# Attention in two layers: the scores a second time, transposed, for one exponential per unit; the band mask on GpSimd

## Chip, cores and metric

The kernel runs on one core of a Trainium2 chip. The metric is the device time of one execution in microseconds (us). The engines run side by side and meet through semaphores: TensorE (PE; its weight loads are PEld), VectorE (DVE), ScalarE (ACT), GpSimd (POOL) and SyncE (SP), which issues most DMAs.

## The reference, cut to what matters

Two blocks follow each other, each with an attention and a feed-forward part; x is (16, 128, 1024).

```
x = x + tanh(g_xattn[0]) * _L0_xattn_ref(_layernorm(x), ctx, ctx, ...)
x = x + tanh(g_ffn[0])   * _L0_ffn_ref(_layernorm(x), ...)
x = x + tanh(g_xattn[1]) * _L1_xattn_ref(_layernorm(x), ctx, ...)
x = x + tanh(g_ffn[1])   * _L1_ffn_ref(_layernorm(x), ...)
# _L0_xattn_ref, per batch, for 16 heads x 4 states (64 "heads" of 16 dimensions), 128 x 128:
scores = einsum('bhqdm,bhkdm->bhqkm', qh, kh) / sqrt(dk)
weights = softmax(scores, axis=3)
out = einsum('bhqkm,bhkdm->bhqdm', weights, vh)
# _L1_xattn_ref: channels as sequence of T = 1024, 8 heads of 16, a window of 16 keys round each query:
dots = einsum('bhdt,bhdtw->bhtw', qh, k_win) * scale     # padded keys are zeros
attn = softmax(dots, axis=-1)
out = einsum('bhtw,bhdtw->bhdt', attn, v_win)
```

## The kernel before

`program` runs seven stages, one after another with a barrier between: setup, `project_q`, `project_kv`, `attention0`, `ffn0_project1`, `attend1`, `select_ffn1`. Both attentions are the function `attend` (lines 725 to 1037). It works in units of 8 heads: layer 0 has 128 units (16 batches of 8) of 128 queries and 128 keys; layer 1 has 144 (16 batches of 9 tiles), a tile being 113 queries (121 in the first, 112 in the last) against the 128 keys that hold their windows.

For a unit u, with the queries on the partitions: `score` (PE) multiplies `qs` and `ks`, both split into high and low parts that lie on 64 partitions, into `s_bank`, 8 matmuls of 128 columns into two of PSUM's banks; in layer 1 two bf16 matmuls of 512 columns first lay down the band of 0 and -1e30. `maximum` (DVE) reduces the 8 rows of scores to their negated maxima `nmax`. `exponential` (ACT) needs one op per head, since its bias is that head's column of `nmax`: 8 ops into `probs`. `turn` (PE) transposes the 8 blocks into `t_bank`; `turn_out` copies them to `pt`, half by DVE and half by ACT. `value` (PE) multiplies them with `vpad`, V padded to 32 columns with a column of ones, so that the sum of each row of probabilities comes along, dimensions on the partitions, into `o_bank`; `value_out` (DVE) copies to `osb`; `turn_back` (PE) transposes that into `b_bank`, queries on the partitions again; `divide` (DVE) takes reciprocals of the sums and multiplies into `att`, which SP stores once a batch. In layer 1 the first and last tile of a batch (edges) also count the padded keys, `raw`, `low`, `epad` and `den`.

The order on each engine is written out by `staggered(eng, units, per_loop, stages)`: in step c, an engine runs its listed functions in order, each for unit c + lead. PE has score at lead 4, turn at 2, value at 1, turn_back at 0, and the other engines have matching lists:

```
staggered(pe, B * upb, un.per_loop, [(4, score), (2, turn), (1, value), (0, turn_back)])
staggered(dve, B * upb, un.per_loop, [(4, maximum), (2, turn_out), (1, value_out), (0, divide)])
staggered(act, B * upb, un.per_loop, [(3, exponential), (2, turn_out)])
```

An engine's list is strictly in order: a wait in it holds everything after it. `done(t)` is the semaphore's value when unit t is finished, `free(t, depth)` when the buffer that unit t reuses is. `s_bank`, `probs` and `pt` have two buffers, `t_bank`, `o_bank` and `b_bank` one. SP loads `qs` and `ks` from DRAM (2 MB for four units of layer 0, 4 MB for a batch of layer 1; two slots) and V, and GpSimd copies V into `vpad` once a batch; in layer 0 it also loads and splits the next stage's weight. `project_kv` (line 579) and `ffn0_project1` (line 1238) write K and Q to DRAM in high and low parts.

## Time and profile before

| | us |
|---|---|
| Median of 3 runs | 2406.85 (2403.96 to 2409.03) |
| The profiled execution | 2407.05, its span 2405.4 |
| PE busy | 2182.1 (91%) |
| DVE busy | 1394.1 (58%) |
| ACT busy | 975.4 (41%) |
| POOL busy | 174.0 (7%) |
| Granted clock of PE, mean | 0.956 of 2.4 GHz |

The page splits the span into 40 slices of 60 us. The stage of layer 0's attention is at slices 12 to 17, that of layer 1's at slices 27 to 34; in both, three engines are busy for most of a slice, outside them ScalarE hardly is. Durations are those of the profiled execution. The end of a matmul is modelled, so for PE the distance from the start of one block to the start of the next is the better measure of what a block takes.

### The profile page before, as it was taken

The numbers are of one execution on the slowest core, as the hardware profiler recorded it, in microseconds if no ns is written. First come the engines' busy times: TensorE is split into PE (matmuls) and PEld (weight loads), VectorE is DVE, ScalarE is ACT, GpSimd is POOL, SyncE is SP. The second block draws the span as 40 slices with busy tenths as digits, with TensorE's granted clock in tenths as the row PEclk, the third lists the DMA queues.
The fourth block names the chain that finished last, engine by engine and source line by source line (L and its number), as shares of the span: only waits on it lengthen the run. The fifth ranks groups of instructions, "written<-read, shape, count | busy, mean of one in ns | idle before, by whom it ended". The sixth has DMA issues, their size and how long they took to land. (4 is left out here: it accounts for less than half of the span.)

```text
span 2405.4 us, 49290 instructions
## 1 busy us (share of the span) xinstructions
PE 2182.1 (91%) x17638; PEld 1766.2 (73%) x17638; DVE 1394.1 (58%) x2604; ACT 975.4 (41%) x2850; POOL 174.0 (7%) x225
## 2 busy tenths in 40 slices
PE   5999699999979999979978999959999996775998
PEld 4999689989957777758854777737777774564887
DVE  4443322112159999923325777649999995784664
ACT  2222221111059999900002111129999995440000
POOL 0000000000021212100000000010000000330000
PEclk9999899999989999989988999979999998886999
DMA  3223533332356777533323878775655653751221
GB/s 126 106 105 123 172 135 132 140 148 113 131 229 260 273 276 267 197 140 131 131 96 128 304 291 314 277 303 183 241 195 195 238 186 96 247 175 58 87 86 58
DMA packets 163583, 426.59 MB, mean 177 GB/s; under 512 B 14192, under 2 KB 90736, under 8 KB 151216
## 3 DMA queue, kind: packets, MB, share of 16 engines
q1 hardware_dynamic: 161200, 417.16, 47.2%
q0 software_dynamic: 2304, 8.39, 1.1%
q8 instruction: 48, 0.79, 0.1%
q14 instruction: 31, 0.25, 0.0%
HBM read 257.73 MB, written 167.77 MB: 177 GB/s over the span
## 5 line engine op out<-in xcount | busy, mean ns | idle before, releaser
L953 ACT ACTIVATE a_probs<-a_s_bank,a_nmax 128x128 f32<-128x128 f32 (+3 forms) x2176 | 598.8, 422 | 36.0 <-DVE a_nmax L893 36.0
L893 DVE TENSOR_REDUCE a_nmax<-a_s_bank 128x8 f32<-128x1024 f32 (+1 forms) x240 | 293.5, 1223 | 47.5 <-PE a_s_bank L999 23.8
L1009 PE MATMUL a_t_bank<-ident_sb,a_probs 128*128 128x128 f32 (+3 forms) x2176 | 286.2, 275 | 1.1 <-ACT a_pt L961 0.8
L1009 PEld LDWEIGHTS a_t_bank<-ident_sb,a_probs 128*128 128x128 f32 (+3 forms) x2176 | 225.0, 142 | 21.0 <-ACT a_probs L953 1.1
L907 DVE COPY a_pt<-a_t_bank 128x512 f32<-128x512 f32 (+3 forms) x272 | 177.1, 651 | 4.3 <-PE a_t_bank L1009 4.3
L961 ACT ACTIVATE a_pt<-a_t_bank 128x512 f32<-128x512 f32 (+3 forms) x272 | 165.0, 606 | 29.0 <-PE a_t_bank L1009 27.4
L1024 PE MATMUL a_o_bank<-a_pt,a_vpad 128*32 128x128 f32 (+3 forms) x4352 | 168.8, 273 | 0.5 <-DVE a_osb L914 0.5
L373 PE MATMUL q_qb<-q_xt_hi,wq_hi 128*128 128x256 f32 x512 | 145.5, 284 | 3.0 <-DVE wq_lo L248 3.0
L373 PE MATMUL kv_kb<-kv_ct_hi,wk_hi 128*128 128x256 f32 x512 | 145.0, 283 | 3.0 <-DVE wv_lo L248 3.0
L373 PE MATMUL kv_kb<-kv_ct_lo,wk_hi 128*128 128x256 f32 x512 | 144.9, 283 | 0.0
L373 PE MATMUL kv_kb<-kv_ct_hi,wk_lo 128*128 128x256 f32 x512 | 144.9, 283 | 0.0
L373 PE MATMUL q_qb<-q_xt_lo,wq_hi 128*128 128x256 f32 x512 | 144.8, 283 | 0.0
L373 PE MATMUL q_qb<-q_xt_hi,wq_lo 128*128 128x256 f32 x512 | 144.8, 283 | 0.0
L1024 PEld LDWEIGHTS a_o_bank<-a_pt,a_vpad 128*32 128x32 f32 x4352 | 99.1, 109 | 42.8 <-issue 23.8
L1351 ACT ACTIVATE f_shared<-f_banks,p_b 128x1024 fp32r<-128x1024 f32 x32 | 35.7, 1116 | 223.8 <-PE f_banks L1400 223.8
L1034 PE MATMUL a_b_bank<-ident_sb,a_osb 128*113 128x128 f32 (+1 forms) x544 | 123.8, 309 | 1.4 <-DVE a_att L936 1.4
L373 PE MATMUL f_banks<-f_hi,f_xt_hi 128*128 128x512 f32 x256 | 105.0, 410 | 7.2 <-DVE f_xt_lo L1295 7.2
L999 PEld LDWEIGHTS a_s_bank<-a_ks,a_qs 64*113 64x113 f32 (+2 forms) x1152 | 69.3, 177 | 57.2 <-issue 57.2
L987 PE MATMUL a_s_bank<-a_band,a_identb 128*113 128x512 bf16 (+2 forms) x288 | 87.2, 385 | 24.9 <-DMA a_ks<-k 22.6
L914 DVE COPY a_osb<-a_o_bank 128x256 f32<-128x256 f32 (+3 forms) x272 | 108.7, 400 | 1.0 <-PE a_o_bank L1024 1.0
L618 DVE TENSOR_TENSOR kv_raw<-kv_vb,bvf 128x512 f32<-128x512 f32 x32 | 22.1, 692 | 149.7 <-PE kv_vb L373 149.7
L612 DVE SCALAR_TENSOR_TENSOR kv_k_lo<-kv_kb,bkf,kv_raw 128x256 fp32r<-128x256 f32 x64 | 31.0, 484 | 133.5 <-ACT kv_raw L639 133.5
(200 smaller groups left out, 4563.6 us busy)
## 6 DMA issues: line engine op xcount, KB each, us to landing
a_qs<-q SPq DMA_DIRECT2D x32, 1024.0 KB, 6.1
a_ks<-k SPq DMA_DIRECT2D x32, 1024.0 KB, 8.1
k<-f_shared SPq DMA_DIRECT2D x64, 512.0 KB, 4.2
a_qs<-q SPq DMA_DIRECT2D x16, 2048.0 KB, 7.8
a_ks<-k SPq DMA_DIRECT2D x16, 2048.0 KB, 11.9
k<-kv_raw SPq DMA_DIRECT2D x32, 512.0 KB, 4.8
k<-kv_k_lo SPq DMA_DIRECT2D x32, 512.0 KB, 4.8
a_vraw<-v SPq DMA_DIRECT2D x32, 512.0 KB, 10.4
```

Of the source, the lines that this page charges most:

```text
L373: m = pe.matmul(out, a(x, c), b(y, c), start=(i + j == 0), stop=(len(terms) * j + i == n - 1))
L893: dve.tensor_reduce(nmax[0:m, k, :], scores(s)[0:m], X, ALU.max, negate=True).then_inc(maxed, 1)
L907: dve.tensor_copy(pt[:, k, 0:512].rearrange("p (h t) -> p h t", h=4)[:, :, 0:m], t_bank[:, 0, :].rearrange("p (h t) -> p h t", h=4)[:, :, ...
L914: dve.tensor_copy(osb[:, k, :].rearrange("p (g t) -> p g t", g=2)[:, :, 0:m], o_bank[:, 0, 0:2 * P].rearrange("p (g t) -> p g t", g=2)[:, ...
L953: a = act.activation(probs[0:m, k, h, :], scores(s)[0:m, h, :], ACT.Exp, bias=nmax[0:m, k, h:h + 1])
L961: act.activation(pt[:, k, 512:1024].rearrange("p (h t) -> p h t", h=4)[:, :, 0:m], t_bank[:, 1, :].rearrange("p (h t) -> p h t", h=4)[:, : ...
L987: pe.matmul(s_bank[0:m, 2 * k + bank, :], identb[:, 0:m], band[:, kind, :, :].rearrange("p h t -> p (h t)"), start=True, stop=False, skip_ ...
L999: a = pe.matmul(out, qs[at, slot, j, t0:t0 + m], ks[at, slot, j, w0:w0 + P], start=False, stop=True, skip_group_check=True)
L1009: a = pe.transpose(t_bank[:, h // 4, h % 4 * P:h % 4 * P + m], probs[0:m, k, h, :], e.ident[0:m, 0:m])
L1024: a = pe.matmul(o_bank[32 * j:32 * j + 32, 0, g * P:g * P + m], vpad[:, slot, UH * (s % upb) + head(h), :], pt[:, k, h * P:h * P + m], sta ...
L1034: a = pe.transpose(b_bank[0:m, 0, g * P:(g + 1) * P], osb[:, k, g * P:g * P + m], e.ident[:])
L1351: act.activation(halves(qk[j][0][:, s % 2, :]), pb, ACT.Identity, bias=b[:, j:j + 1]).then_inc(hi[j], 1)
```

## The change

In both attentions each unit's scores are computed twice. The first pass is as before, but with one buffer and only for the maxima. The maxima of a group of units (4 in layer 0, 3 in layer 1) are transposed by PE (`turn_max`), copied by ACT (`shift`) and written by a DMA that ACT issues into the rows 0 and 64 of `qs`, which are high parts' partners of rows of ones in `ks`: one DMA per group in layer 0, one per tile in layer 1. The second pass (`score_t`) has keys on the partitions and the queries as columns, and subtracts the maxima by those rows; one exponential per unit then writes `pt` directly. `turn`, `probs` and both `turn_out` go. `value_out` moves from DVE to ACT. In layer 1 the band is applied to `pt` after the exponential by GpSimd (`mask`), a multiplication of the bits, as integers, with 0 or 1; the band matmuls of the first pass stay. Tiles of layer 1 have 112 queries (120 in the first and last). `pt` has three buffers in layer 1, `qs` and `ks` four slots. The pipeline is deeper: score runs 9 units ahead. DRAM's K gets rows of ones, written in setup, and K is stored in five pieces instead of four, with the order of high and low parts swapped. The stores of layer 1's `att` are three instead of five. Values and division stay as they were in form.

```diff
 WIN, PADL = 16, 8
-TSTEP = P - WIN + 1
+TSTEP = P - WIN
 NT1 = 9
 NCL = 64
 QS = 0.25
 RAW = 4
-START = 16
+START = 32
...
+K_ROWS = ((0, slice(1, 16)), (0, slice(17, 32)), (1, slice(0, 32)), (2, slice(0, 32)), (3, slice(0, 32)))
+Q_ROWS = ((0, slice(0, 32)), (1, slice(0, 32)))
...
+            sp.wait_ge(unit_set, 1)
+            for k in (e.k0, e.k1):
+                sp.dma_start(k[:, 0:32:16, 0, :], unit[:]).then_inc(unit_out, 16)
+            sp.wait_ge(unit_out, 32)
+
+        @block.gpsimd
+        def _(pool):
+            pool.memset(unit[:], 1.0).then_inc(unit_set, 1)
...
-                    for j in range(4):
-                        sp.dma_start(e.k0[2 * g + b][:, j, :],
-                                     (k_hi, k_lo)[j % 2][:, b].rearrange("p o t -> p (o t)").bitcast(F32)
-                                     ).then_inc(k_out, 16)
+                    for j, r in K_ROWS:
+                        src = (k_lo, k_hi)[j % 2][4 * r.start:4 * r.stop, b].rearrange("p o t -> p (o t)")
+                        sp.dma_start(e.k0[2 * g + b][r, j, :], src.bitcast(F32)).then_inc(k_out, 16)
...
+        self.group = 4 if layer == 0 else 3
+        self.per_loop = 16 if layer == 0 else 36
+        self.batches = self.per_loop // self.per_batch
+        self.groups = self.per_loop // self.group
+        self.ahead = self.group + 4
...
+    G, L, upb = un.group, un.ahead, un.per_batch
+    R = UH * G
+    E = layer
+    D3 = 2 + E
...
-        s_bank = ps(n + "s_bank", [P, 4, 512]); t_bank = ps(n + "t_bank", [P, 2, 512])
-        o_bank = ps(n + "o_bank", [P, 1, 512]); b_bank = ps(n + "b_bank", [P, 1, 512])
-        v_zeroed = sem(n + "v_zeroed"); const = sem(n + "const")
-        qk_in = [sem(n + f"qk_in{k}") for k in range(2)]
+        s_bank = ps(n + "s_bank", [P, 2, 512]); st_bank = ps(n + "st_bank", [P, 4, 512])
+        b_bank = ps(n + "b_bank", [P, 1, 512]); o_bank = ps(n + "o_bank", [P, 1, 512])
...
+                slot, b = s // 4, un.batches * i + s // NU
+                sp.wait_ge(st_done, done(u - 13))
...
-                staggered(sp, B * upb, un.per_loop, [(0, store), (upb + 1, load_half), (upb + 1, load_values)])
+                staggered(sp, B * upb, un.per_loop, [(0, store), (14, load_half), (10, load_values)])
             else:
-                staggered(sp, B * upb, un.per_loop, [(0, store), (upb + 5, load_batch), (upb + 5, load_values)])
+                staggered(sp, B * upb, un.per_loop, [(0, store), (18, load_batch), (14, load_values)])
...
+            def mask(u, s, i):
+                m = un.rows(s)
+                kind = {None: 1, 0: 0, 1: 2}[un.edge(s)]
+                pool.wait_ge(expd, done(u))
+                p = pt[:, s % D3, :, 0:m]
+                pool.tensor_tensor(p.bitcast(I32), p.bitcast(I32), bandi[:, kind, 0:m].unsqueeze(1).to_broadcast([P, UH, m]),
+                                   ALU.mult).then_inc(masked, 1)
...
+            staggered(pool, B * upb, un.per_loop, [(2, mask), (6, batch_values)])
...
             def maximum(u, s, i):
-                m, k = un.rows(s), s % 2
+                m = un.rows(s)
                 dve.wait_ge(scored, done(u))
-                dve.wait_ge(expd, free(u))
+                to = nmax[0:m, s // G % 2, :].rearrange("p (a x) -> p a x", a=2)
+                if layer == 0:
+                    to = to[:, :, 4 * (s % 4):4 * (s % 4) + 4]
+                else:
+                    to = to.rearrange("p a (j t) -> p a t j", t=G)[:, :, s % G, :]
                 if un.edge(s) is None:
-                    dve.tensor_reduce(nmax[0:m, k, :], scores(s)[0:m], X, ALU.max, negate=True).then_inc(maxed, 1)
+                    dve.tensor_reduce(to, s_bank[0:m].rearrange("p b (h x) -> p b h x", h=4), X, ALU.max,
...
-            def turn_out(u, s, i):
-                m, k = un.rows(s), s % 2
-                dve.wait_ge(turned, done(u))
-                dve.wait_ge(valued, free(u))
-                dve.tensor_copy(pt[:, k, 0:512].rearrange("p (h t) -> p h t", h=4)[:, :, 0:m],
...
-            staggered(dve, B * upb, un.per_loop, [(4, maximum), (2, turn_out), (1, value_out), (0, divide)])
+            staggered(dve, B * upb, un.per_loop, [(L + 1 + E, maximum), (0, divide)])
...
             def exponential(u, s, i):
                 m, k = un.rows(s), s % 2
-                act.wait_ge(maxed, done(u))
-                act.wait_ge(turned, free(u))
-                if un.edge(s) is not None:
-                    act.activation(epad[0:m, un.edge(s), :], low[0:m, un.edge(s), :], ACT.Exp)
-                for h in range(UH):
-                    a = act.activation(probs[0:m, k, h, :], scores(s)[0:m, h, :], ACT.Exp,
-                                       bias=nmax[0:m, k, h:h + 1])
-                a.then_inc(expd, 1)
-
-            def turn_out(u, s, i):
+                act.wait_ge(st_done, done(u))
+                act.wait_ge(valued, free(u, D3))
+                act.activation(pt[:, s % D3, :, 0:m], by_head(st_bank[:, 2 * k:2 * k + 2, :])[:, :, 0:m],
+                               ACT.Exp).then_inc(expd, 1)
+
+            def shift(u, s, i):
+                if not un.group_last(s):
+                    return
+                g, k, mg = un.nth_group(s, i), s // G % 2, un.group_rows(s)
+                nth = un.groups // 2 * i + s // G // 2
+                act.wait_ge(turned, g + 1)
+                act.wait_ge(shift_in[k], 16 * shifts * nth)
+                act.activation(nrow[:, k, 0:mg], b_bank[0:R, 0, 2 * P:2 * P + mg], ACT.Copy).then_inc(rowed, 1)
+                act.wait_ge(rowed, g + 1)
+                if layer == 0:
+                    act.dma_start(qs[0:65:64, s // 4, :, :].bitcast(F32), nrow[:, k, :].bitcast(F32)).then_inc(shift_in[k], 16)
+                    return
+                for tile in range(G):
+                    slot, js, q, _ = place(s - s % G + tile)
+                    act.dma_start(qs[0:65:64, slot, :, q].bitcast(F32),
+                                  nrow[tile:R:G, k, 0:q.stop - q.start].bitcast(F32)).then_inc(shift_in[k], 16)
+
+            def value_out(u, s, i):
...
+            staggered(act, B * upb, un.per_loop, [(L + E, shift), (2 + E, exponential), (1, value_out), (4, pads)])
...
-                pe.wait_ge(expd, free(u))
+                elif un.first(s):
+                    pe.wait_ge(qk_in[slot], 32 * (i + 1))
+                pe.wait_ge(maxed, free(u, 1))
...
+            def turn_max(u, s, i):
+                if not un.group_last(s):
+                    return
+                g, mg = un.nth_group(s, i), un.group_rows(s)
+                pe.wait_ge(maxed, done(u))
+                pe.wait_ge(normed, done(u - L - E - 1))
+                pe.transpose(b_bank[0:R, 0, 2 * P:2 * P + mg], nmax[0:mg, s // G % 2, :].bitcast(F32),
+                             e.ident[0:mg, 0:mg]).then_inc(turned, 1)
+
+            def score_t(u, s, i):
+                slot, js, q, k = place(s)
+                m, st = un.rows(s), 2 * (s % 2)
+                if un.group_first(s):
+                    nth = un.groups // 2 * i + s // G // 2
+                    pe.wait_ge(shift_in[s // G % 2], 16 * shifts * (nth + 1))
+                pe.wait_ge(expd, free(u))
+                for j in range(4):
+                    for half in range(2):
+                        at = slice(64 * half, 64 * half + 64)
+                        a = pe.matmul(st_bank[:, st + half, j * P:j * P + m], ks[at, slot, js.start + j, k],
+                                      qs[at, slot, js.start + j, q], start=True, stop=True,
+                                      skip_group_check=True)
+                a.then_inc(st_done, 1)
...
-            staggered(pe, B * upb, un.per_loop, [(4, score), (2, turn), (1, value), (0, turn_back)])
+            staggered(pe, B * upb, un.per_loop, [(L + 1 + E, score), (2 + E, score_t), (L + E, turn_max), (1, value), (0, turn_back)])
```

## Rows read from the trace of the kernel before

**Rows 1.** The page's GB/s per slice; busy us (and count) by window, granted clock, DMA share, GB/s.
```profile
GB/s 126 106 105 123 172 135 132 140 148 113 131 229 260 273 276 267 197 140 131 131 96 128 304 291 314 277 303 183 241 195 195 238 186 96 247 175 58 87 86 58
...
core 0: us, PE busy (x) PEld busy (x) DVE busy (x) ACT busy (x) POOL busy (x), PEclk, DMA share, GB/s
...
700.00:1000.00 300.00, 296.69 (x3920) 226.13 (x3918) 289.35 (x579) 297.07 (x1044) 59.34 (x56) 0.99 0.70 264
...
1620.00:2000.00 380.00, 380.00 (x4836) 275.46 (x4828) 346.49 (x762) 356.27 (x1241) 19.14 (x30) 1.00 0.54 196
```
**Rows 2.** Timeline, first score block and last store of each attention stage: start us, duration us.
```profile
686.84 1.97 PE L995 MATMUL a_s_bank<-a_ks,a_qs 64*128 64x128 f32 x16 [12.36 <-DMA a_ks<-k]
...
1027.38 0.35 SPq L833 DMA_DIRECT2D att<-a_att  x1
...
1604.98 1.08 PE L987 MATMUL a_s_bank<-a_band,a_identb 128*121 128x512 bf16 x2 [22.65 <-DMA a_ks<-k]
...
2021.70 2.51 SPq L841 DMA_DIRECT2D att<-a_att  x5
```
**Rows 3.** Timeline of a step in layer 0's attention, PE and ACT.
```profile
802.19 0.65 ACT L961 ACTIVATE a_pt<-a_t_bank 128x512 f32<-128x512 f32 x1
...
802.66 0.44 PE L1034 MATMUL a_b_bank<-ident_sb,a_osb 128*128 128x128 f32 x2
802.68 2.22 ACT L953 ACTIVATE a_probs<-a_s_bank,a_nmax 128x128 f32<-128x128 f32 x8
...
803.03 0.66 PE L995 MATMUL a_s_bank<-a_ks,a_qs 64*128 64x128 f32 x8
...
803.62 1.09 PE L1009 MATMUL a_t_bank<-ident_sb,a_probs 128*128 128x128 f32 x8
...
804.64 0.65 PE L1024 MATMUL a_o_bank<-a_pt,a_vpad 128*32 128x128 f32 x16
...
805.22 0.44 PE L1034 MATMUL a_b_bank<-ident_sb,a_osb 128*128 128x128 f32 x2
```
**Rows 4.** Timeline of a step in layer 1's attention, PE and the maximum on DVE.
```profile
1801.58 0.59 PE L987 MATMUL a_s_bank<-a_band,a_identb 128*113 128x512 bf16 x2
...
1802.10 0.61 PE L999 MATMUL a_s_bank<-a_ks,a_qs 64*113 64x128 f32 x8
...
1802.64 0.99 PE L1009 MATMUL a_t_bank<-ident_sb,a_probs 113*128 113x113 f32 x8
1802.75 1.22 DVE L893 TENSOR_REDUCE a_nmax<-a_s_bank 113x8 f32<-113x1024 f32 x1 [0.32 <-PE a_s_bank L999]
...
1803.56 0.59 PE L1024 MATMUL a_o_bank<-a_pt,a_vpad 128*32 128x113 f32 x16
...
1804.09 0.47 PE L1034 MATMUL a_b_bank<-ident_sb,a_osb 128*113 128x128 f32 x2
...
1804.40 0.59 PE L987 MATMUL a_s_bank<-a_band,a_identb 128*113 128x512 bf16 x2
```
**Rows 5.** Timeline where layer 0's attention drains, with engines waiting.
```profile
1023.46 0.60 ACT L961 ACTIVATE a_pt<-a_t_bank 128x512 f32<-128x512 f32 x1 [1.25 <-PE a_t_bank L1009]
...
1024.07 0.42 DVE L914 COPY a_osb<-a_o_bank 128x256 f32<-128x256 f32 x1
...
1024.64 0.64 PE L1024 MATMUL a_o_bank<-a_pt,a_vpad 128*32 128x128 f32 x16 [0.27 <-DVE a_osb L914]
```
**Rows 6.** Groups by line and form: count, busy us in all, mean ns of one.
```profile
L1148 ACT ACTIVATE wo_xt_hi<-wo_tb 128x1024 fp32r<-128x1024 f32 x16 | 16.4, 1026 | 181.6 <-PE wo_tb L1164 181.6
...
L900 DVE TENSOR_SCALAR a_nmax<-a_raw,a_edges 112x8 f32<-112x8 f32 x15 | 3.4, 225 | 0.0
...
L360 POOL TENSOR_TENSOR wo_lo<-wo_raw,wo_hi 128x1024 f32 x8 | 18.9, 2359 | 0.0
```
**Rows 7.** Timeline of SyncE's queue in layer 1's attention, five stores of `att`.
```profile
1644.40 3.08 SPq L841 DMA_DIRECT2D att<-a_att  x5
```
**Rows 8.** By tile: landing of layer 0's `att` stores, then of GpSimd's `wo_raw` loads.
```profile
DMA to landing us min/median/max: 2.6/2.9/3.5
...
DMA to landing us min/median/max: 3.7/3.9/8.3
```

285 lines of the change are left out of this document (148 added, 137 removed).

## Prediction

> **What bounds the kernel now.** I read the page first: its rows of slices show that the work runs stage after stage (projections, attention of layer 0, a product, the low-rank product, attention of layer 1, selection, last product), so a change in one stage is worth what it does in that stage. The change touches the two attention stages. Busy time by window [rows 1] shows TensorE (PE) at 296.7 of 300 us of the first and 380.0 of 380 us of the second, at a granted clock of 0.99 and 1.00 of 2.4 GHz. ScalarE (297.1, 356.3) and VectorE (289.4, 346.5) are nearly as full, so no engine's time can be read as free until the others are counted. The stages last from their first score matmul to their last `att`: 686.8 to 1027.4 = 340.6 us, and 1605.0 to 2021.7 = 416.7 us [rows 2].
>
> Then the timeline of one step, where every PE block starts as the one before ends. Layer 0 [rows 3]: turn back 0.37 us (802.66 to 803.03), score 0.59, turn of the probabilities 1.02, value 0.58; a step is 2.56 us. Layer 1 [rows 4]: band matmuls 0.52, score 0.54, turn 0.92, value 0.53, turn back 0.31; a step is 2.82 us. With PE never idle, PE is the engine that sets the step, and the other two keep pace.
>
> **The change, part by part.**
>
> *PE, steady step.* The turn goes; a second score pass of the same form (eight 64-row matmuls) comes. Layer 0: its price is the score's 0.59, so a step is 0.58 + 0.37 + 0.59 + 0.59 = 2.13 us. Layer 1: between 0.54 and 0.59 [rows 3, 4]; I take 0.57, since the stationary side is 128 wide as in layer 0 and 112 columns move: 0.52 + 0.54 + 0.57 + 0.53 + 0.31 = 2.47 us. Once in a group (4 units in layer 0, 3 in layer 1) a small transpose of the maxima is added, half of the two-transpose turn back, 0.19 us. PE alone would give 2.18 and 2.53 us.
>
> *The maximum.* The scores now have one buffer, so score(u+1) waits for maximum(u), and all PE work queues behind it. The maximum starts 0.65 us after the score block starts and takes 1.23 [rows 4]; from the end of a VectorE op to the PE block that waits for it there are 0.15 us, of which the weight load takes the last 0.03 (1024.49 to 1024.64, [rows 5]); I use 0.12. Layer 0: 0.70 + 1.23 + 0.12 = 2.05, under 2.13, hidden with 0.08 to spare. Layer 1: 0.52 + 0.65 + 1.23 + 0.12 = 2.52, over 2.47, so a plain step is 2.52. Edge tiles (2 of 9) do one more small op of 0.225 [rows 6] before they report; in the one that doesn't fall in a slower step anyway this costs 0.33, or 0.04 a unit. VectorE loses both of its copies and keeps the maximum and two short ops: its sum is no bound.
>
> *ScalarE, throughput.* Eight exponentials and half of the copy become one exponential of 1024 (896) columns and the copy of the values. ScalarE takes 0.60 us for 512 columns and 1.026 for 1024 [rows 5, 6], so 0.92 for 896, 0.39 for 256, 0.36 for 224, and 0.28 for the 120 or 128 of the maxima. The next op starts 0.11 us before such a copy would end by itself: 0.49 after its start [rows 3]. That gives slots of 0.92 and 0.81 us for the exponential. About 1.3 us a step: no bound by its sum.
>
> *ScalarE, order.* This is the term that decides. Once a group ScalarE waits for the transpose of the maxima, which PE does in the middle of its step, copies the row (0.28), waits for that copy, and issues the DMA that puts it into `qs`: one in layer 0, three in layer 1. Behind it stand the exponential of that step and the copy of the values, and for that copy wait the next value block and turn back on PE. No row shows a DMA issued by ScalarE. SyncE's own: five stores with fixed addresses take 2.51 us, 0.50 each [rows 2]. Bounds are 0.35, the bare duration of one store [rows 2], and 0.62, five with computed addresses in 3.08 us [rows 7]. The addresses of the new DMAs are fixed: 0.50. With T the start of a group step on PE:
> Layer 0: score and second score to 1.18, transpose to 1.37, seen at 1.48; copied 1.81; issued 2.31; exponential to 3.23; values copied 3.62; seen by PE at 3.74. PE is ready for the next value block at 2.32 + 1.18 = 3.50. Stall 0.24. Average (4 x 2.13 + 0.19 + 0.24) / 4 = 2.24 us.
> Layer 1: band, score and second score to 1.63, transpose to 1.82, seen 1.93; copied 2.26; three issues to 3.76; exponential to 4.57; values copied 4.93; seen 5.05. PE is ready at 2.66 + 1.63 = 4.29. Stall 0.76. Average (2.66 + 2.47 + 0.76 + 2.52) / 3 = 2.80, with the edges 2.84 us. So layer 1's step stays at today's 2.82, although its matmuls shrink. With issues of 0.35 and 0.62 it would be 2.70 and 2.96.
>
> *GpSimd.* Layer 1's mask is one tensor_tensor of 896 columns per unit, behind the exponential and ahead of the value matmuls. The nearest row, two inputs and 1024 columns, takes 2.36 us [rows 6]: 2.06 for 896. The copy of V into its pad, 1152 columns a batch, adds at most 2.65 / 9 = 0.29. Some 2.4 us with waits, under 2.84; exponential to value has over two steps of room, as `pt` has three buffers. This row is fp32 and the mask is int32; a gain is excluded (the two reads stay), a loss isn't. The Trainium skill ("GPSIMD Engine Reference", Engine selection) advises against two-input elementwise work on this engine, as VectorE does it about twice as fast; by it the mask belongs on VectorE. The row says the mask fits, so the sum leaves it free; the rule's case is the first rival.
>
> *DMA.* The maxima arrive as 16 KB (layer 0), issued by T + 2.3 and needed by the second score three steps on, at about T + 7.3: 5.0 us; in layer 1 5.6 us. Stores of 512 KB land in 2.6 to 3.5 us [rows 8]. Layer 0's loads are the same bytes in less time: 264 GB/s [rows 1] becomes about 300, while single slices of the page show up to 314 [rows 1]. Hidden; a miss is the second rival. The five K stores instead of four, and the rows of ones in setup, lie on SyncE's queue beside PE work of other stages; I take 0, bounds 0 and 3 us.
>
> *Ends of the stages.* The pipeline is 9 units deep instead of 4. In the fill, PE mostly does scores alone, one maximum apart, and at about half speed, as in today's first blocks: band 1.08 us instead of 0.59 [rows 2, 4]. Layer 0: about 2.45 us a step, 22 in all; layer 1: six of 3.4 and three of 2.6, 28. Drain: layer 0 seven steps of 1.54 and two of 1.8, 14.4 us; layer 1 is held to GpSimd's 2.2 a unit, 18.
>
> *Sum.* Of the 128 + 9 and 144 + 9 steps, 119 and 135 are full ones. Layer 0: 22 + 119 x 2.24 + 14.4 = 303.0, against 340.6: -37.6. Layer 1: 28 + 135 x 2.84 + 18 = 429.4, against 416.7: +12.7. The rest: 0. Net -25: the profiled execution's 2407.05 (span 2405.4 and 1.65 around it; 0.2 above the median of the runs) gives 2382 us.
>
> **Rivals.**
> *The mask is slower than its fp32 relative* (a slower-ending case). GpSimd then sets layer 1's step from 2.5 us a mask on. At 3.2 us a step is about 3.5: 28 + 135 x 3.5 + 22 = 523 against 429, time 2476. For it: an integer product was never seen in this trace. Against: reading two inputs likely limits the row, not its arithmetic. Chance 0.15.
> *The maxima land late.* Each us beyond 5 costs 32 us in layer 0 (32 groups) and, beyond 5.6, 48 in layer 1. Landing in 6 us: 2382 + 32 + 19 = 2433. For it: a GpSimd load of 512 KB issued beside the first loads of the stage took 8.3 us. Against: the other loads of that line took 3.9 in the median beside loads as well [rows 8], and these transfers are 32 times smaller. Chance 0.12.
> *ScalarE's issues cost little* (0.1 us each). Layer 1's stall goes and its step is 2.61: 398 us, 31 less; layer 0 saves another 7: time 2344. Chance 0.15.
> *It doesn't do what it says*: the step stays PE's and PE does not speed up, because the second pass with weights 128 wide costs what the turn did (1.02, 0.92). Then 2.6 and 2.9 us: layer 0 346, layer 1 438, time 2434. Against: the first pass has the same form. Chance 0.05.
>
> **How the numbers follow.** Forecast 0.53, rivals as above. The forecast's own range, from the bounds of the issue (layer 1 -19 and +16, layer 0 -4 and +4), the fill (10 either way) and the K stores: 2350 to 2412. With the cheap issue below and the late landing above, 2338 to 2434 leaves out the slow mask and little else. Faster by over 0.2% (4.8 us, about what a measurement of this kernel can tell): 0.47 of the forecast, 0.15 of the cheap issue, 0.08 of a mask or a landing that misses only a little, 0.70. Same 0.08. Slower 0.22.
>
> **What the profile would show.** Layer 0's PE blocks at 2.13 us with a gap of 0.2 before every fourth value block; in layer 1 a gap of 0.8 before every third, released by ScalarE's copy of the values, with ScalarE standing in DMA issues before it. `nmax` reduce follows score at once. GpSimd at some 80% in layer 1 with masks near 2.1 us. Wrong if PE waits for the mask, if it waits for `qs` from `nrow`, if layer 1's stage is under 400 us, or if another stage moves by over 5 us.

## The result, and the profile after

The changed kernel takes 2722.75 us (median of 4 runs, 2705.31 to 2739.22), the kernel before 2407.94 beside it (4 runs, 2403.96 to 2410.29): 1.131 times as long, interval 1.123 to 1.138. The forecast was 2382 us, and the wider of its two ranges ended at 2434. The profiled execution spans 2716.1 us, 310.7 more than before.

The page of the changed kernel: its span, the busy sums, and of the slices the rows of PE, ACT, POOL, the clock and the DMA rate.

```profile
span 2716.1 us, 46746 instructions
...
PE 2429.7 (89%) x17718; PEld 1919.8 (71%) x17718; DVE 1210.9 (45%) x2060; ACT 640.9 (24%) x1026; POOL 476.2 (18%) x373
...
PE   5997899999799999979968999499888989685999
...
ACT  1221311110243434400001111023333333242000
POOL 0000000000211111100000000045565555332000
PEclk9999999999555555579989999657687575686999
...
GB/s 127 94 139 120 144 164 112 168 95 149 237 191 202 188 185 202 94 133 130 108 146 182 301 304 288 338 90 153 133 167 150 128 151 81 172 224 101 63 93 62
```

The row to stop at is PEclk, the clock that TensorE was granted, in tenths of 2.4 GHz. PE is as full in layer 0's attention (slices 10 to 16, counted from 0) as it was, but the clock is at 5 tenths for seven slices in a row, and it wanders between 5 and 8 in layer 1's (slices 26 to 34). Busy time by window, layer 0's stage and then layer 1's; columns as in [rows 1]:

```profile
686.60:1161.70 475.10, 463.91 (x4384) 344.21 (x4384) 220.52 (x384) 184.70 (x288) 66.26 (x63) 0.50 0.47 181
1743.70:2332.80 589.10, 527.42 (x5232) 360.48 (x5232) 290.77 (x528) 191.21 (x368) 322.12 (x176) 0.64 0.38 138
```

Layer 0's stage is 475.1 us instead of 340.6 [rows 2], at 0.50 of 2.4 GHz, the level of 1.2 GHz, instead of 0.99 [rows 1]: +134.5. Layer 1's is 589.1 instead of 416.7, at 0.64 instead of 1.00: +172.4. Together 306.9 of the 310.7 us; all the rest adds 3.8. PE is not waiting: from 720 to 1140 us it is busy for 420.00 of 420 us, at 0.50 throughout. ScalarE went from 297 busy us of 300 [rows 1] to 185 of 475, and VectorE from 289 of 300 to 221 of 475. The change did to them what it says.

A step of layer 0 in the timeline (start, duration):

```profile
900.35 0.69 PE L1117 MATMUL a_b_bank<-ident_sb,a_osb 128*128 128x128 f32 x2
...
900.97 1.11 PE L1065 MATMUL a_s_bank<-a_ks,a_qs 64*128 64x128 f32 x8
...
901.89 1.05 PE L1089 MATMUL a_st_bank<-a_qs,a_ks 64*128 64x128 f32 x8
...
902.87 1.08 PE L1103 MATMUL a_o_bank<-a_pt,a_vpad 128*32 128x128 f32 x16
902.98 1.02 ACT L1004 ACTIVATE a_pt<-a_st_bank 128x1024 f32<-128x1024 f32 x1 [2.11 <-PE a_st_bank L1089]
...
903.88 0.69 PE L1117 MATMUL a_b_bank<-ident_sb,a_osb 128*128 128x128 f32 x2
```

The four blocks are the forecast ones, back to back, and ScalarE had waited 2.11 us before its exponential. But each block takes 1.6 to 1.7 times its old length: score 0.92 (900.97 to 901.89) for 0.59, turn back 0.62 for 0.37, value 1.01 for 0.58 [rows 3]; the second score takes 0.98. The step is 3.53 us where 2.13 was forecast. It is PE's own clock, not a wait.

A group step of layer 1, in a stretch where the clock was up:

```profile
1986.95 0.25 ACT L1014 ACTIVATE a_nrow<-a_b_bank 24x112 fp32r<-24x112 f32 x1 [2.57 <-PE a_b_bank L1076]
1987.24 1.61 ACTq L1021 DMA_DIRECT2D a_qs<-a_nrow  x3
...
1989.01 0.97 ACT L1004 ACTIVATE a_pt<-a_st_bank 128x960 f32<-128x960 f32 x1 [1.81 <-issue]
1989.88 0.35 ACT L1028 ACTIVATE a_osb<-a_o_bank 128x224 f32<-128x224 f32 x1
1990.06 6.31 POOL L930 TENSOR_TENSOR a_pt<-a_pt,a_bandi 128x960 int32<-128x960 int32 x3 [3.79 <-ACT a_pt L1004]
...
1990.38 0.62 PE L1103 MATMUL a_o_bank<-a_pt,a_vpad 128*32 128x120 f32 x16 [1.17 <-ACT a_osb L1028]
```

This is the forecast's chain, line for line: row copied, three issues, exponential, values copied, and PE at the value block having waited for that copy: 1.17 us, forecast 0.76. (The tile in this step has 120 queries, hence 960 columns; the clock had come up at 1986.2 us.) By form, the masks: 2088 ns for 896 columns, 2.06 forecast.

```profile
L930 POOL TENSOR_TENSOR a_pt<-a_pt,a_bandi 128x896 int32<-128x896 int32 x112 | 232.1, 2088 | 166.4 <-ACT a_pt L1004 166.2
```

### The profile page after: what moved, and what is told of

Its sections match the earlier page's. It is cut to its first block and busy times, and to the rows that moved or that the text cites. A ratio compares the mean times of both kernels' runs of the same rounds, so it can differ in the third digit from the quotient of the medians.

```text
span 2716.1 us, 46746 instructions
## 1 busy us (share of the span) xinstructions
PE 2429.7 (89%) x17718; PEld 1919.8 (71%) x17718; DVE 1210.9 (45%) x2060; ACT 640.9 (24%) x1026; POOL 476.2 (18%) x373
## 5 line engine op out<-in xcount | busy, mean ns | idle before, releaser
L957 DVE TENSOR_REDUCE a_nmax<-a_s_bank 128x8 fp32r<-128x1024 f32 (+1 forms) x240 | 293.9, 1225 | 206.7 <-PE a_s_bank L1065 206.7
L1004 ACT ACTIVATE a_pt<-a_st_bank 128x1024 f32<-128x1024 f32 (+2 forms) x272 | 264.8, 974 | 417.8 <-PE a_st_bank L1089 307.2
L930 POOL TENSOR_TENSOR a_pt<-a_pt,a_bandi 128x896 int32<-128x896 int32 (+1 forms) x144 | 302.4, 2118 | 261.4 <-ACT a_pt L1004 261.0
L1065 PEld LDWEIGHTS a_s_bank<-a_ks,a_qs 64*128 64x128 f32 (+2 forms) x2176 | 220.8, 284 | 158.9 <-issue 150.0
L1065 PE MATMUL a_s_bank<-a_ks,a_qs 64*128 64x128 f32 (+2 forms) x2176 | 268.8, 390 | 26.0 <-DMA a_ks<-k 12.4
L1103 PE MATMUL a_o_bank<-a_pt,a_vpad 128*32 128x128 f32 (+2 forms) x4352 | 258.8, 381 | 17.1 <-ACT a_osb L1028 16.6
L1089 PE MATMUL a_st_bank<-a_qs,a_ks 64*128 64x128 f32 (+2 forms) x2176 | 261.9, 383 | 6.2 <-DMA a_qs<-a_nrow 6.2
L1089 PEld LDWEIGHTS a_st_bank<-a_qs,a_ks 64*128 64x128 f32 x2176 | 239.3, 301 | 11.4 <-issue 6.0
L1117 PE MATMUL a_b_bank<-ident_sb,a_osb 128*112 128x128 f32 (+1 forms) x544 | 172.5, 416 | 1.4 <-DVE a_att L990 1.4
L1059 PE MATMUL a_s_bank<-a_band,a_identb 128*112 128x512 bf16 (+1 forms) x288 | 131.3, 552 | 46.2 <-DMA a_ks<-k 25.2
```

Source lines behind the costliest of these rows:

```text
L930: pool.tensor_tensor(p.bitcast(I32), p.bitcast(I32), bandi[:, kind, 0:m].unsqueeze(1).to_broadcast([P, UH, m]), ALU.mult).then_inc(masked, 1)
L957: dve.tensor_reduce(to, s_bank[0:m].rearrange("p b (h x) -> p b h x", h=4), X, ALU.max, negate=True).then_inc(maxed, 1)
L1004: act.activation(pt[:, s % D3, :, 0:m], by_head(st_bank[:, 2 * k:2 * k + 2, :])[:, :, 0:m], ACT.Exp).then_inc(expd, 1)
L1059: pe.matmul(s_bank[0:m, bank, :], identb[:, 0:m], band[:, kind, :, :].rearrange("p h t -> p (h t)"), start=True, stop=False, skip_group_ch ...
L1065: a = pe.matmul(s_bank[0:m, half, j * P:(j + 1) * P], qs[at, slot, js.start + j, q], ks[at, slot, js.start + j, k], start=layer == 0, stop ...
L1089: a = pe.matmul(st_bank[:, st + half, j * P:j * P + m], ks[at, slot, js.start + j, k], qs[at, slot, js.start + j, q], start=True, stop=Tru ...
```

## The experiments

My theory after the first look: the granted clock falls because the turn of the probabilities is gone. It was PE's longest block, eight fp32 transposes on all 128 rows and columns of the array; what takes its place has matmuls on 64 rows. (Two such transposes stay, in the turn back, and in layer 1 the band matmuls, bf16 on 128 by 128.) Rivals: the level is lost at the stage's start and a push would bring it back; the stalls in the steps pull it down; the missing work of ScalarE and VectorE has to do with it.

For each kernel: its time, and length in us and granted clock of both attention stages. e4 and e8 are edits of the kernel before, all others of the changed one. From e1 to e12 each is one execution. The kernel before took 2404 to 2412 us in all of its executions beside them.

| kernel | time | layer 0 | layer 1 |
|---|---|---|---|
| before | 2407.94 | 340.6, 0.98 | 416.7, 0.99 |
| after | 2722.75 | 475.1, 0.50 | 589.1, 0.64 |
| e4_halfturn | 2520.56 | 455.7, 0.50 | 416.7, 0.99 |
| e8_quarterturn | 2434.97 | 364.3, 0.88 | 417.6, 0.98 |
| e1_fill4 | 2920.54 | 620.4, 0.51 | 641.9, 0.73 |
| e2_warm | 2725.86 | 482.5, 0.51 | 596.5, 0.62 |
| e3_fillb1 | 2766.05 | 566.5, 0.50 | 541.1, 0.84 |
| e5_fillb4 | 2695.91 | 423.7, 0.96 | 618.0, 0.88 |
| e6_warm_fillb1 | 2789.13 | 586.2, 0.51 | 549.7, 0.86 |
| e7_warm_fillb2 | 2593.17 | 387.4, 0.95 | 562.0, 0.90 |
| e13_repeat (the same kernel) | 2611.1, 4 runs | 387.5, 0.95 | 576.2, 0.87 |
| e9_nomask | 2825.9 | 631.5, 0.52 | 548.2, 0.92 |
| e10_sp | 2757.97 | 631.0, 0.52 | 477.6, 0.98 |
| e11_sp_plain | 2638.88 | 474.9, 0.50 | 511.8, 0.75 |
| e12_sp_fill31 | 2594.97 | 424.8, 0.93 | 518.2, 0.83 |

**e4_halfturn**, the decisive one, takes the kernel before and changes the turn's form alone. The form is three things at once: 64 rows instead of 128, plain matmuls instead of transposes, and fp32r operands instead of fp32 (the declarations of `probs` and of the summed identity `identr` are not shown). It leaves out half of each transposition:

```diff
+                for h in (0, 4, 1, 5, 2, 6, 3, 7):
+                    if layer == 0:
+                        at = slice(64 * (h // 4), 64 * (h // 4) + 64)
+                        a = pe.matmul(t_bank[:, h // 4, h % 4 * P:h % 4 * P + m], probs[at, k, h, :], identr[at, :],
+                                      start=True, stop=True, skip_group_check=True)
```

> The kernel before, with one thing changed in layer 0's attention: the eight matmuls of the turn take 64 rows (one half of the queries twice over, so half of the transposition is left out) in the form of the score matmuls, instead of 128 rows of fp32. All waits, copies, exponentials and DMAs are as before, and less is computed on TensorE. Theory C: the granted clock in layer 0's attention falls to about 0.5, its step goes from 2.56 to about 3.5 us, and the time rises by about 125 us to 2530 us, while layer 1 stays at 417 us. Rival S: the clock stays near 1.00, the step stays at 2.56 us, where ScalarE and VectorE hold it, and the time is 2400 to 2410 us.

2520.56 us; layer 0 went from 340.6 to 455.7, layer 1 stayed at 416.7. A window inside layer 0, in the kernel before and in e4:

```profile
800.00:1000.00 200.00, 198.19 (x2636) 151.12 (x2628) 194.07 (x389) 199.51 (x702) 37.32 (x37) 1.00 0.71 267
```

```profile
850.00:1050.00 200.00, 200.00 (x1934) 150.69 (x1932) 155.74 (x284) 151.77 (x511) 30.58 (x30) 0.50 0.50 192
```

Same engines, buffers and DMAs, the same order but for that of the eight matmuls; PE is busy for 198.2 and 200.0 of 200 us, with 27% fewer matmuls in the same time, and the clock is at 1.00 in one and 0.50 in the other. Its step is the 3.53 us of the changed kernel:

```profile
899.96 1.08 PE L1034 MATMUL a_o_bank<-a_pt,a_vpad 128*32 128x128 f32 x16
...
901.59 1.11 PE L1000 MATMUL a_s_bank<-a_ks,a_qs 64*128 64x128 f32 x8
902.51 1.05 PE L1016 MATMUL a_t_bank<-a_identr,a_probs 64*128 64x128 f32 x8
903.49 1.08 PE L1034 MATMUL a_o_bank<-a_pt,a_vpad 128*32 128x128 f32 x16
```

ScalarE still does its eight exponentials here, so their loss isn't the cause; the form of the turn alone does it. Which of the three things in it counts isn't shown, and layer 1's turn was left as it was, so for layer 1 the cause is carried over.

**e8_quarterturn** does so for four of the eight transposes of a unit (each of the four leaves out half its queries).

```diff
+                    if layer == 0 and h % 4 < 2:
```

> The kernel before with four of layer 0's eight turn matmuls in the 64-row form and four in the old one (the former leave out half of their queries). Theory C: the amount of full-array work decides, so this lies between: either the clock still holds (time 2405 us, step 2.56 us, since ScalarE and VectorE hold it) or it falls and the step is 1.2 GHz's, about 4.2 us by blocks of 0.7, 1.1, 1.6 and 1.1 us, at most 2640 us. It fell to 0.50 with none of them (e4). I expect it to fall for at least part of the stage: time 2450 to 2600 us. Rival F (the clock went down in e4 for the form of these matmuls, not for the loss of full-array work): 0.50 throughout, as in e4, 2520 to 2640 us.

364.3 us: the clock was low for 99 us, from before the stage's first matmul to 780.0 us, the 89.5th of the stage, and then at 1.00 to the stage's end. So the level is not a question of yes or no about the whole turn: in this one execution, half of it brought the clock back, late.

**e2_warm** tests the start: 48 transposes of 128 by 128 ahead of the first score.

```diff
+            for _ in range(48):
+                pe.transpose(s_bank[:, 0, 0:P], e.ident[:], e.ident[:])
```

> The changed kernel with 48 identity transposes ahead of the first score of each attention stage, while the loads are under way, so that TensorE is busy without a gap before the pipeline starts; nothing is added to the steps. Theory C1 (the clock only has to be brought up once; the steps would hold it): layer 0 runs at a granted clock of 1.00 with steps of 2.24 us, 305 us instead of 475, and the time is 2400 to 2450 us. Theory C2 (the steps themselves don't hold it): the clock falls back within some tens of us and the time is 2710 to 2735 us. Rival S: the same as C2, without a stretch of faster steps at the start.

2725.86 us, unchanged. The clock rose for 7 us and then stayed at half for 492. It fell at 694.2 us, between the second and the third score of the stage, and their rows show why the test is weaker than meant:

```profile
692.40 0.66 PE L1067 MATMUL a_s_bank<-a_ks,a_qs 64*128 64x128 f32 x8 [1.40 <-DVE a_nmax L957]
694.38 1.12 PE L1067 MATMUL a_s_bank<-a_ks,a_qs 64*128 64x128 f32 x8 [1.32 <-DVE a_nmax L957]
```

In the fill PE waits 1.0 to 1.4 us for each maximum. The clock was gone before the first full step, so whether full steps would hold it was not tested; what the run shows is that they don't bring it back (PE busy for 420.00 of 420 us from 720 to 1140, at 0.50).

The traces say the same of every fall. In all fifteen, whenever the clock fell in an attention stage, PE had been idle for at least 1.2 of the ten us before. None shows it falling out of a stretch without idle time, though not all idle time made it fall. So the turn's part, as far as it is shown, is in bringing the clock back after the idle time of a stage's start.

**Fillers.** If the kind of work that PE does decides, useless full-array work in each unit must bring the clock back. Two forms were tried ahead of the second score: fp32 transposes of the identity (e1), and bf16 matmuls of 128 by 128 weights with 512 columns (e3, e5, e6, e7). e1:

```diff
+                for _ in range(4):
+                    pe.transpose(st_bank[:, st, 0:P], e.ident[:], e.ident[:])
```

> The changed kernel with four more matmuls per unit on TensorE that compute nothing: transposes of the 128 x 128 fp32 identity, the form of the old turn, put into the score bank just ahead of the second score pass, which overwrites them. Work is only added. Theory C (the stages are slow because TensorE's clock is granted at 1.2 GHz, and it stays there because the turn, the only block of matmuls that uses all 128 rows and columns, is gone): the clock comes back to 2.4 GHz, layer 0's step is 2.24 + 0.51 = 2.75 us and its stage 370 instead of 475 us, layer 1's step 3.35 us and its stage 498 instead of 589; time 2526 us. Rival S (the stages are slow by their waits: the issue of the DMAs by ScalarE, the mask, the single score buffer; the clock follows from them): the added work only adds, 1.02 us a step at 1.2 GHz; time 2850 to 3000 us.

2920.54 us, which is in the rival's range and far from my theory's, and layer 0 stayed at 0.51. Four transposes are half of what the turn had, 0.51 us of its 1.02 [rows 3], and as many as e8 kept; but e8 has 12 matmuls on 64 rows beside them in a step, e1 has 16. What each instruction weighs can't be told from this.

```diff
+                for _ in range(1):
+                    pe.matmul(st_bank[:, st, :], fillb[:, 0, :], fillb[:].rearrange("p a t -> p (a t)"), start=True, stop=True,
+                              skip_group_check=True)
```

That is e3, cold. e5 has four of them, cold; e6 one and e7 two, both after e2's warm-up and with four such matmuls beside each score of the fill.

> The changed kernel with one bf16 matmul of 128 x 128 weights and 512 columns per unit ahead of the second score pass, which computes nothing: a cheaper full-array filler, 0.26 us at 2.4 GHz by the band matmuls (0.52 for two). Theory C: if this much is enough, layer 0's step is 2.50 and its stage 338 us, layer 1's step 3.10 and its stage 465 us, time 2461 us; if it isn't, the clock stays at 0.50 in layer 0 and the time is 2722 + 137 x 0.45 + 153 x 0.4 = 2845 us. Rival S: 2845 us as well, with the clock unchanged, and no faster steps.

> The changed kernel with four bf16 matmuls (128 x 128 weights, 512 columns) per unit ahead of the second score pass, 0.84 us a step at 2.4 GHz and 1.7 at 1.2; they compute nothing. One of them (e3) left layer 0 at a clock of 0.50. Theory C (full-array columns per time keep the clock up): layer 0's attention is granted 1.00 after its fill, its step is 2.13 + 0.84 + 0.05 = 3.02 us and the stage about 400 us, against 475 without the added work; layer 1's step 3.3 to 3.5 us, stage 480 to 520 against 589; time 2530 to 2570 us. Rival H (the clock is held down by something other than a lack of full-array work, such as the two transfers per group or the drain between blocks): clock 0.50, 5.2 us a step in layer 0, 710 us, time 3000 us or more.

> The changed kernel with 48 identity transposes ahead of the first score, four bf16 matmuls of 512 columns in each step of the fill, and one in each later step. Theory B (two stable states: at 1.2 GHz the steps are longer, so the same filler is a smaller share of them; brought up first, the clock then stays up): layer 0 at 1.00 with steps of 2.50 us, stage 345 us; layer 1 3.0 us and 450 us; time 2450 to 2480 us. Rival T (one filler isn't enough at either clock): as e3_fillb1 from shortly after the fill on, layer 0 at 0.50 to 0.6 and time 2740 to 2780 us.

> As e6_warm_fillb1 with two bf16 matmuls in each later step. Theory C with two states: layer 0 at 1.00, steps of 2.60 us (2.13 + 0.42 + 0.05), stage 360 us; layer 1 3.1 us, stage 465; time 2470 to 2490 us. Rival T: two fillers don't hold it either, layer 0 near 0.5 with steps of 4.4 us, 600 us, time 2850 us.

One filler left layer 0's clock at 0.50, warmed up or not (e6: 0.51, low for 594 us). My idea in e6, that a warm start would be kept with little work, was not tested either: there too the clock fell in the fill, at 696.6 us. With four fillers it came back after 41 us at the low level and stayed for 393; with two and the warm-up, after 34 us, for 345. In layer 1 a single filler made the stage shorter, 541.1 us at 0.84 (e3) for 589.1 at 0.64. There the step already holds two bf16 matmuls of 512 columns, the band's, the form of e7's two fillers; that may be why layer 1's clock wanders and doesn't stay low, but no run takes them away. The times of e5 and e7 lay over 100 us above what I expected, because of layer 1 (below). e7's steps in layer 0, at the full clock:

```profile
903.49 0.66 PE L1074 MATMUL a_s_bank<-a_ks,a_qs 64*128 64x128 f32 x8
904.08 0.61 PE L1096 MATMUL a_st_bank<-a_fillb 128*128 128x512 bf16 x2
904.62 0.66 PE L1101 MATMUL a_st_bank<-a_qs,a_ks 64*128 64x128 f32 x8
905.21 0.64 PE L1115 MATMUL a_o_bank<-a_pt,a_vpad 128*32 128x128 f32 x16
905.78 0.44 PE L1129 MATMUL a_b_bank<-ident_sb,a_osb 128*128 128x128 f32 x2
906.15 0.66 PE L1074 MATMUL a_s_bank<-a_ks,a_qs 64*128 64x128 f32 x8
```

The step is 2.66 us with 0.54 of fillers in it: 2.12 without, where 2.13 was forecast. The step arithmetic was right, at a clock that the changed kernel doesn't get. It also shows why fillers save nothing: 2.66 is more than today's 2.56.

**e13_repeat** runs e7's kernel again, because e9 and e10, with the same work for PE in layer 0, had stayed at half clock there.

> The kernel of e7_warm_fillb2 again, in several executions. Its layer 0 was at the full clock for 345 us (387.4 us, time 2593), while e9_nomask and e10_sp, whose layer 0 does the same work, had it at half for 601 us (631.5 and 631.0). Theory A (near the edge the level is decided anew in each execution): the times fall into two bundles some 244 us apart, about 2593 and 2837. Theory B (the small differences of those programs decide): all executions within 1% of 2593.

Three executions took 2593.56, 2605.97 and 2616.23 us, one 2877.14 at a mean clock of 0.829 (0.928 in the profiled one). So one program took two times some 270 us apart. The traces kept (e7's and that of 2616.23) both have layer 0 at 387 us and differ in layer 1, 562.0 against 576.2. That of 2877.14 isn't kept; that it lost its time in layer 0 is argued from e9 and e10, whose clock stayed low there for 601 us and whose layer 0 is 244 us longer. Their layer 0 is therefore not compared with e7's. (e9 and e10 ran on another chip than e7 and e13; but e13's four executions shared one.)

```profile
800.00:1000.00 200.00, 200.00 (x2671) 129.15 (x2659) 126.30 (x222) 100.23 (x166) 38.68 (x36) 1.00 0.66 257
```

```profile
800.00:1000.00 200.00, 200.00 (x1521) 121.30 (x1523) 72.39 (x126) 60.73 (x95) 25.00 (x24) 0.50 0.37 143
```

The first window is e13's, the second e9's: the same PE instructions, PE busy for 200.00 of 200 us in both, 2671 against 1521 matmuls.

**Layer 1: what is not the clock.** With bf16 fillers the clock was 0.84 to 0.90 in layer 1 and the stage still took 541 to 618 us. e7's waits of PE there (us in total, times, longest):

```profile
PE a_st_bank L1096 <- DMA a_qs<-a_nrow: 23.1, 11, 4.5
PE a_o_bank L1115 <- ACT a_osb L1030: 20.2, 37, 1.9
```

The second is the forecast's stall; the first is the late landing, a rival at 0.12 (L1096 is the filler, which stands where the second score waits). **e10_sp** moves the issues from ScalarE to SyncE:

```diff
+            def issue(u, s, i):
+                ...
+                sp.wait_ge(rowed, g + 1)
...
+                        sp.dma_start(qs[0:65:64, slot, :, q].bitcast(F32),
+                                      nrow[tile:R:G, k, 0:q.stop - q.start].bitcast(F32)).then_inc(shift_in[k], 16)
...
-                        act.dma_start(qs[0:65:64, slot, :, q].bitcast(F32),
```

> The kernel of e7_warm_fillb2 (2593.17 us; layer 0 387.4, layer 1 562.0), but the DMAs that carry the maxima are issued by SyncE at the same place in its list, not by ScalarE; ScalarE only copies the row. Theory A (the issues on ScalarE hold the copy of the values, and through it PE, once a group): in layer 1 three issues of 0.52 us leave ScalarE and the stall of about 1.2 us before every third value block goes: 48 groups x 0.8 to 1.2 = 38 to 58 us, of which some returns in other waits: layer 1 falls by 20 to 45 us. In layer 0 one issue a group: 32 x 0.24 = 8 us at most, 0 to 8. Time 2545 to 2573. Theory B (the maxima's landing sets the pace in layer 1, whoever issues them; SyncE has q, k, v loads and stores in its queue ahead): layer 1 within 10 us of 562 or longer, and PE's waits for the rows in qs grow from 48 us.

Layer 1: 477.6 us against 562.0 and 576.2, twice what I expected at most. Both waits are gone from PE's list, whose largest is now 5.9 us. PE's idle time fell from 61.8 (562.0 less 500.2) to 19.0 (477.6 less 458.6) and its busy time by 41.6, at a clock of 0.98 instead of 0.90. So about half of the 84 us were the stalls; the other half came with the higher clock. Windows of both stages, e7 and e10:

```profile
1651.60:2213.60 562.00, 500.18 (x5553) 300.40 (x5551) 274.63 (x528) 186.52 (x368) 323.44 (x176) 0.90 0.40 143
```

```profile
1893.00:2370.60 477.60, 458.59 (x5553) 280.67 (x5551) 268.14 (x528) 180.80 (x368) 325.07 (x176) 0.98 0.46 168
```

That the interruptions cost the clock can be read inside e10. Its clock fell twice in mid-stage, at 2038.0 and 2154.0 us. The first two windows are the ten us before each fall, the third is from the stretch in which it did not fall:

```profile
2028.00:2038.00 10.00, 7.00 (x86) 4.34 (x86) 4.37 (x11) 2.53 (x5) 6.40 (x3) 1.00 0.22 57
2144.00:2154.00 10.00, 7.11 (x84) 4.22 (x85) 4.57 (x11) 3.15 (x6) 6.40 (x3) 1.00 0.16 42
2170.00:2365.00 195.00, 194.20 (x2463) 120.35 (x2461) 114.75 (x232) 82.39 (x168) 147.54 (x80) 1.00 0.42 152
```

**e11_sp_plain** makes that move alone in the changed kernel.

> The changed kernel (2722.75 us; attention of layer 0 475.1, of layer 1 589.1 at a clock of 0.64) with one edit: SyncE issues the DMAs of the maxima; no filler, no warm-up. In e10_sp, with fillers, layer 1 fell from 562.0 to 477.6 and its clock rose from 0.90 to 0.98. Theory A (layer 1's clock falls because stalls interrupt PE; without them it stays high): layer 1 at 2.5 us a step, 144 x 2.5 + 40 = 400 us, clock over 0.9, time about 2535. Theory B (as in layer 0, the loss of the full-array turn leaves PE's work too light whether it is interrupted or not): layer 1's clock stays between 0.5 and 0.75; without stalls 144 steps at 2.44 / 0.6 = 4.1 us less what is not at the low level: 500 to 600 us, time 2630 to 2740. Layer 0: 475 within 10 in both.

2638.88 us, 84 less than the changed kernel (one execution; the changed kernel's four span 34 us). Layer 1 fell from 589.1 to 511.8, its clock rose from 0.64 to 0.75 only: theory B's values. Two things act there: PE's idle time, of which 45.4 us are left (511.8 less 466.4) and after which the clock falls, and steps that bring it back late (it was low for 58 to 79 us three times). Layer 0 is as before the edit (474.9).

**e12_sp_fill31** adds one filler in layer 1 and three in layer 0.

> SyncE issues the DMAs of the maxima, warm-up as in e7_warm_fillb2, three full-array filler matmuls per unit in layer 0 and one in layer 1. Layer 0: two fillers gave 387 us in one run and 631 in two others, four gave 424. If the level depends on how heavy the steps are, three hold it: 128 x 2.93 + 28 = 403 us at a clock of 0.95 or more; if it is chance, 403 or about 690. Layer 1: one filler gives a PE step of 2.44 + 0.27 = 2.71 us: at the full clock 144 x 2.71 + 35 = 425 us, no longer than the 416.7 of before by more than 2%; if one filler is too little for the clock, 500 or more. Time: 2465 where both hold, over 2540 where one does not.

Layer 0 held the clock after 58 us: 424.8. Layer 1 didn't with one filler: 0.83, up for 27 to 116 us at a time and down for 3 to 79 in between; 518.2 us. Its step at the full clock was 2.76 us (2101.06 to 2103.82, band to band), and 144 of them are 397 us without the fill, so even at that clock layer 1 would be near today's 416.7 (an estimate). No version beat the kernel before.

**e9_nomask** takes the mask from GpSimd in e7's kernel; it leaves out the band on the probabilities.

```diff
-                pe.wait_ge(masked if layer else expd, done(u))
+                pe.wait_ge(expd, done(u))
...
-            staggered(pool, B * upb, un.per_loop, [(2, mask), (6, batch_values)])
+            staggered(pool, B * upb, un.per_loop, [(6, batch_values)])
```

> The changed kernel with the warm-up and the two full-array filler matmuls per unit of e7_warm_fillb2 (2593.17 us; layer 0's attention 387.4 us, layer 1's 562.0 at a granted clock of 0.90), but GpSimd does no mask: the value matmuls wait for the exponential alone. It leaves out the band on the probabilities of layer 1. Theory A (the mask costs through VectorE: its short edge ops stand up to 2 us beside a running mask, and maxima and score blocks queue behind them): layer 1 falls by 20 to 40 us, to 522 to 542, the time to 2553 to 2573; VectorE's two short edge ops are back at 0.17 to 0.23 us. Theory B (GpSimd is off the path, as forecast, and layer 1's excess comes from the order on ScalarE and from late maxima): layer 1 stays within 10 us of 562. Layer 0 has no mask and stays at 387 in both.

Layer 1 took 548.2, 14 less than e7's 562.0, itself 14 from its repeat's 576.2: neither theory's value. In e7's kernel the mask costs at most some 14 to 28 us, and nothing that I can tell from the spread. In the changed kernel, which e9 doesn't test, its trace is clear. VectorE's two short edge ops beside the masks of above, which ran from 1990.06 to 1996.37:

```profile
1993.65 0.71 DVE L964 TENSOR_SCALAR a_nmax<-a_raw,a_edges 120x8 fp32r<-120x8 f32 x1
1994.40 2.00 DVE L967 TENSOR_SCALAR a_low<-a_nmax 120x8 f32<-120x8 f32 x1
1994.42 0.18 PEld L1059 LDWEIGHTS a_s_bank<-a_band,a_identb 128*120 128x120 bf16 x2 [0.95 <-DVE a_nmax L964]
...
1996.80 0.29 DVE L990 TENSOR_TENSOR a_att<-a_b_bank,a_rinv 120x128 f32<-120x128 f32 x1
...
1997.23 0.26 PE L1076 MATMUL a_b_bank<-ident_sb,a_nmax 120*24 120x120 f32 x1 [1.17 <-DVE a_att L990]
```

They take 0.23 and 0.17 us without a mask beside them (e9's means by form). Here the first ended at 1994.36 and the second at 1996.40, near the ends of the second and third mask, and PE waited for the first. Behind the second stood the division (L990), and PE waited 1.17 us for that before it could transpose the maxima. In layer 1 of the changed kernel PE waited 12.2 us in all, 9 times, for this division and 8.6 us for the first edge op (L964), together more than the 16.6 us for the copy of the values. In e7, where the second edge op keeps its 0.17 us, the wait for the division is not in the list; in e11, where it is long again (0.81 in the mean), the wait is 13.0 us. The Trainium skill ("SBUF — State Buffer", Who interferes with whom) says that a tensor_scalar of VectorE in its two-port mode and a GpSimd instruction take turns on a shared port, whole instructions at a time; these rows agree, though none shows in which mode the two ops ran. In e10 the same ops have means of 233 and 172 ns beside all the masks: there the mask of a step ended just before them (2119.89 + 2.09 = 2121.98; the edge op began at 2122.06). So whether the mask hurts depends on the moment in the step at which it runs.

## Why the prediction was wrong, point by point

**The step that failed** stands in the first part and was never a term of the sum: "at a granted clock of 0.99 and 1.00 of 2.4 GHz". I took block lengths from rows at that level, 0.59 for a score pass, 0.58, 0.37, and carried them into a PE that has lost its turn. I let the fill run at half speed, and let the clock come back by itself, as it did in today's first blocks. It doesn't: in layer 0 of the changed kernel the clock stays at 1.2 GHz to the end. In the kernel before it came back with the turn in its old form, and didn't when e4 changed that form alone: +115.1 of layer 0's 134.5 us; the other 19.4 weren't taken apart. In the forecast's own terms: 3.53 us a step for 2.13, and 475.1 us for 303.0.

I read "With PE never idle, PE is the engine that sets the step" as a reason to take work off PE, and took its clock for given. For layer 1 the 172.4 us are not taken apart by one run: e11 shows 77.3 of them to come with ScalarE's issues, by their stalls and the clock; that the rest has layer 0's cause is argued.

The Trainium skill ("TensorE: Matmul & The Clock Gate", HAM oscillation) puts the low level down to gaps in which PE is idle. On how the clock falls the traces agree: idle time came before every fall, in e2 gaps of 1.3 and 1.4 us. They don't on why it stays low. In layer 0 PE is busy for 420.00 of 420 us, and in e4 for 200.00 of 200, at 0.50; gaps don't explain that, and the measurement decides.

**PE's steady step at the full clock**: right. 2.12 in layer 0 (e7), forecast 2.13. In layer 1, e10's step is 2.97 us (2101.31 to 2104.28, band to band) with 0.54 of fillers: 2.43, forecast 2.47. With the maximum in the chain, plain steps of the changed kernel were 2.46 and 2.50 us, forecast 2.52, and PE's weight load waited 0.25 us for `nmax` in one of them (2004.49).

**ScalarE's issue**: right in size, for all 144 and 32 of them 0.515 to 0.518 us in the median, forecast 0.50. **The stall behind it**: right in place and order, too small: 1.17 for 0.76 in the group step shown. The exponential began 0.16 us after the last issue's end (1988.85 to 1989.01), and the rest of the difference wasn't taken apart. It mostly vanishes over the whole stage, most of which runs at half clock, where PE is slower and ScalarE isn't: 16.6 us in all, 17 times, in layer 1 of the changed kernel. What I had not seen is its second price, the clock (e10, e11).

**The maxima's landing**: 0.8 us of waiting in layer 0 and 5.4 in layer 1 of the changed kernel. Right there; in e7, at nearly the full clock, it is 23.1 us, up to 4.5 at a time. The slack of 5.6 us was too small there; with SyncE as issuer the wait is gone.

**The mask**: 2.09 us for 2.06, and 0.3 us of waiting for it in the whole stage: right, and the first rival (0.15) fell. Its effect on VectorE's short ops was not in the forecast: the edge tiles were priced at 0.04 us a unit, some 6 us a stage, and PE waited 20.8 us for the edge op and the division.

**The second pass costs what the turn did** (0.05): its block did, 0.98 against 1.02, yet for another reason than the rival's. By its form it costs 0.59 as the first pass does (e7); the clock makes 0.98 of it, and of every other block too much as well, so the rival's 2434 us fell.

**Ends of stages, K stores, loads**: the other stages moved by 3.8 us in all (4.4 longer between the two attentions, 0.6 shorter around them). The fills can't be read at the forecast's clock. DMA of layer 0 fell to 181 GB/s instead of rising to 300, since PE was slower.

What the sum would have been at the clock it took for granted can be estimated from e7 and e10. Layer 0: 387.4 less 128 x 0.54 of fillers, less some 14 us for the 34 at the low level (a step there is 2.66 x 2663 / 1521 = 4.66, by the matmuls of e7 and e9 in 200 us), is 304, forecast 303. Layer 1 with SyncE's issues: 477.6 less 144 x 0.54 is 400, under today's 416.7. That a kernel with both would gain 50 us is argued, not shown: the clock was up for most of a stage only in kernels that have the fillers which I subtract.

**What stays open**: what of a PE instruction counts for the level, and whether steady steps without the turn would hold a clock that was up when they began, in layer 0. Per unit of layer 0, with four fp32 transposes or one bf16 matmul added the clock stayed low; with two it came back in some executions and not in others; with three and with four it came back, in one execution each. Chances: I gave 0.22 to slower and none of it to this mechanism; the range ended 289 us short.

## What to carry to other kernels

Treat the granted clock as a term of the sum. Before full-array matmuls are taken out of a stage that runs at 1.00, or replaced by ones of another form, price the stage at the low level too (here 1.6 to 1.7 times the step), for PE busy all the time is no sign that the clock is up. Changing the form of that one block in the old kernel, as e4 does, tests it by itself. Look at what PE does at the stage's start as well: there the clock fell, in the kernel before too, and the kernels differ in whether it came back. And put the DMA issues of a serial chain on a queue where nothing that PE needs stands behind them: layer 1 became 84 us (e10) and 77 us (e11) shorter when 144 issues of 0.5 us left ScalarE.

## What the hardware showed that I had not expected

- A PE that is busy all the time at 0.50: 420.00 of 420 us in the changed kernel (720 to 1140), 560.00 of 560 in e9 and e10 (720 to 1280). The matmul blocks are 1.6 to 1.7 times as long there, not twice.
- The level is not a function of the program alone: one kernel took 2593 to 2616 us in three executions and 2877 in a fourth.
- The clock fell in an attention stage only after idle time of PE, at least 1.2 of the ten us before, in all fifteen traces. In layer 1 it rose from 0.90 to 0.98 when 43 us of idle time went out of 562 (e7, e10).
- A VectorE op of 0.17 us took 2.00 beside a GpSimd op of two inputs, and 0.17 beside the same ones in another phase.
